# Swin attention and a spiking layer on one core: the softmax's exponentials over both score banks in one operation each

## The reference, cut to what matters

```python
qkv = (part @ qkv_w.T + qkv_b).reshape(n * NW, WS, 3, N_HEAD, HEAD_DIM)
q, k, v = (qkv[:, :, 0] * SCALE, qkv[:, :, 1], qkv[:, :, 2])
attn = jnp.einsum('wihd,wjhd->whij', q, k)
attn = attn.reshape(n, NW, N_HEAD, WS, WS) + bias[None, None] + MASK[None, :, None]
attn = jax.nn.softmax(attn, axis=-1).reshape(n * NW, N_HEAD, WS, WS)
out = jnp.einsum('whij,wjhd->wihd', attn, v).reshape(n * NW, WS, c)
...
x = x + _L0_conv_ref(_gn(x), L0_conv_qkv_w, L0_conv_qkv_b, L0_conv_bias_table)
x = x + _L1_conv_ref(_gn(x), L1_conv_W, L1_conv_b)
```

## Time and profile before

| what | value |
| --- | --- |
| median of 3 runs | 576.61 us (572.59 to 577.72) |
| profiled execution | 574.5 us |
| its span | 572.8 us |
| granted TensorE clock, mean over the span | 0.951 of full speed |

### The profile page before, as it was taken

One profiled execution on the slowest core, in us unless ns is written; L12 is line 12 of the kernel. 1 busy time (PEld: TensorE's weight loads), 2 busy tenths in 40 slices (PEclk: granted clock), 3 DMA queues, 4 the chain that ended last, 5 costly groups with the idle time before them and its releaser, 6 DMA issues.

```text
span 572.8 us, 18181 instructions
## 1 busy us (share of the span) xinstructions
PE 470.8 (82%) x6632; PEld 426.5 (74%) x6632; DVE 464.0 (81%) x995; ACT 434.2 (76%) x1045; POOL 318.1 (56%) x411
## 2 busy tenths in 40 slices
PE   0364699898999899899989998998999778599880
PEld 0364588787888788788878887887888667599770
DVE  6855568888898789888888987898778775779997
ACT  2275679888898899888888988998889567579830
POOL 6133365566555666655566656566555466867630
PEclk9978799999999999999999999999999898889975
DMA  6266066666777677666667776765565450221233
GB/s 185 73 171 160 15 168 173 175 167 181 190 200 192 165 189 180 165 174 170 181 168 196 193 190 167 186 153 150 155 154 153 132 148 3 92 75 74 97 116 137
DMA packets 92577, 86.09 MB, mean 150 GB/s; under 512 B 41842, under 2 KB 63604, under 8 KB 92532
## 3 DMA queue, kind: packets, MB, share of 16 engines
q1 hardware_dynamic: 91808, 85.49, 55.8%
q10 hardware_dynamic: 724, 0.01, 0.1%
HBM read 47.72 MB, written 33.55 MB: 142 GB/s over the span
## 4 chain that ended last, share of the span: by engine, by line
issue 26%; POOL 24%; PE 21%; DVE 11%; ACT 8%; DMA 6%; SPq 2%; POOLq 1%; ACTq 1%; DVEq 0%
POOL p_lo L426 11%; POOL xc L413 5%; POOL xn_lo L386 3%; DVE xc L865 3%; PE pv_ps L1009 3%; DMA k_stack<-k_spill1lo 2%; ACT v_hi L508 2%; DMA k_spill1lo<-k_lo 2%; PE proj_ps L909 2%; PE proj_ps L911 2%; PE proj_ps L910 2%; PE score_ps L986 2%; DVE charged L857 2%; DMA probs<-in_qkv_b_dram 1%; PE max_ps L953 1%
## 5 line engine op out<-in xcount | busy, mean ns | idle before, releaser
L426 POOL TENSOR_TENSOR p_lo<-probs,p_hi 128x512 f16<-128x512 f32 x128 | 146.7, 1167 | 162.6 <-ACT p_hi L587 162.6
L909 PE MATMUL proj_ps<-xn_hi,w_hi 128*128 128x256 f32 x288 | 86.1, 299 | 14.6 <-POOL xn_lo L386 14.0
L763 DVE TENSOR_TENSOR v_lo<-proj_ps,v_hi 64x128 f16<-64x128 f32 x256 | 74.1, 289 | 22.5 <-ACT v_hi L508 19.8
L586 ACT ACTIVATE probs<-score_ps 128x512 f32<-128x512 f32 x128 | 76.9, 601 | 18.1 <-PE score_ps L986 17.3
L976 PE MATMUL score_ps<-both_parts,bias_k 128*128 128x64 f16 x1024 | 82.6, 194 | 6.2 <-DMA k_stack<-k_spill1lo 4.3
L910 PE MATMUL proj_ps<-xn_lo,w_hi 128*128 128x256 f32 x288 | 83.1, 288 | 0.0
L911 PE MATMUL proj_ps<-xn_hi,w_lo 128*128 128x256 f32 x288 | 83.0, 288 | 0.0
L770 DVE TENSOR_REDUCE neg_max<-max_ps 128x16 f16<-128x1024 f32 x64 | 78.4, 1225 | 4.7 <-PE max_ps L959 2.7
L386 POOL TENSOR_TENSOR xn_lo<-xn,xn_hi 128x512 fp32r<-128x512 f32 x48 | 62.5, 1302 | 34.8 <-ACT xn_hi L480 34.7
L978 PE MATMUL score_ps<-q_stack,k_stack 96*128 96x64 f16 x1024 | 81.8, 193 | 0.0
L472 ACT ACTIVATE xn<-xc,shift,rstd 128x256 f32 (+1 forms) x128 | 70.6, 611 | 12.9 <-DVE shift L238 6.6
(11 more groups left out here) (144 smaller groups left out, 1434.9 us busy)
## 6 DMA issues: line engine op xcount, KB each, us to landing
xc<-in_x_dram SPq DMA_DIRECT2D x32, 256.0 KB, 4.9
k_stack<-k_spill0hi SPq DMA_DIRECT2D x32, 256.0 KB, 4.2
k_stack<-k_spill1hi SPq DMA_DIRECT2D x32, 256.0 KB, 4.1
out_dram<-xc SPq DMA_DIRECT2D x32, 256.0 KB, 2.3
q_hi<-q_flat SPq DMA_DIRECT2D x128, 32.0 KB, 2.0
k_spill0hi<-k_hi SPq DMA_DIRECT2D x16, 256.0 KB, 2.2
k_spill0lo<-k_lo SPq DMA_DIRECT2D x16, 256.0 KB, 2.4
q_stack<-q_spill0hi SPq DMA_DIRECT2D x32, 128.0 KB, 2.8
```

What stands on the lines that cost most here:

```text
L426: pool.tensor_tensor(p_lo[p][:, quads, :, :].rearrange("p g w i -> p (g w i)"), probs[:, quads, :, :].rearrange("p g w i -> p (g w i)"), p ...
L586: act.activation(probs[:, quads, :, :].rearrange("p g w i -> p (g w i)"), score_ps[:, h, :], ACT.Exp)
L909: pe.matmul(dst, w_hi[:, c, cols], high[:, tok], start=(c == 0 and bias is None), stop=False)
```

## The change

Each of the two exponentials runs once a pair, over both banks of `score_ps` (1024 columns), in place of once a bank. `p_hi_done` counts pairs, and no longer halves. ACT's exponentials therefore wait for both increments of `score_ps_done`, and for both low parts of the pair before; POOL's first low part waits for the whole f16 exponential; PE's scores of the next pair wait for the whole exponential of this one, for the first bank too. POOL's operations keep their size, two of 512 columns a pair.

```diff
--- before.py
+++ after.py
@@ -421,7 +421,7 @@
                 wait(pool, pv_ps_done, n - 1)
                 for h in range(HALVES):
-                    pool.wait_ge(p_hi_done, n * 2 + (h + 1))
+                    pool.wait_ge(p_hi_done, n + 1)
                     quads = slice(h * QUADS, (h + 1) * QUADS)
@@ -579,13 +579,11 @@
                 wait(act, pv_ps_done, n - 1)
-                for h in range(HALVES):
-                    wait(act, p_lo_done, n * 2 + (h - 1))
-                    act.wait_ge(score_ps_done, n * 2 + (h + 1))
-                    quads = slice(h * QUADS, (h + 1) * QUADS)
-                    act.activation(probs[:, quads, :, :].rearrange("p g w i -> p (g w i)"), score_ps[:, h, :], ACT.Exp)
-                    act.activation(p_hi[p][:, quads, :, :].rearrange("p g w i -> p (g w i)"), score_ps[:, h, :], ACT.Exp)\
-                       .then_inc(p_hi_done, 1)
+                wait(act, p_lo_done, n * 2)
+                act.wait_ge(score_ps_done, n * 2 + 2)
+                both_banks = score_ps[:, :, :].rearrange("p h n -> p (h n)")
+                act.activation(probs[:, :, :, :].rearrange("p g w i -> p (g w i)"), both_banks, ACT.Exp)
+                act.activation(p_hi[p][:, :, :, :].rearrange("p g w i -> p (g w i)"), both_banks, ACT.Exp).then_inc(p_hi_done, 1)
@@ -968,7 +966,7 @@
                 for h in range(HALVES):
-                    wait(pe, p_hi_done, n * 2 + (h - 1))
+                    wait(pe, p_hi_done, n)
                     for g in range(QUADS):
```

## The result

The changed kernel takes 585.67 us (median of 6 runs, 584.07 to 589.08), the kernel before 576.07 in the runs beside it (572.59 to 577.72). The ratio is 1.0187, 95% interval 1.0141 to 1.0234: 1.9% slower, 9.6 us between the medians. (A ratio leaves out every run that is more than 1.5% above the fastest run of its own kernel; here that happened twice, at 590.80 and 590.63 us, both in the kernel with the gap filled.) The profiled execution took 585.46 us, its span 583.7 against 572.8: 10.9 us more. (Behind the two exponentials, lines of the changed kernel carry numbers lower by two: L907 is `project_q`'s first matmul, L701 the root guess.)

What follows compares the result with a forecast made beforehand. Ordinary rows were taken as bound by PE's projections and ACT's `k_hi`, `max_rows`, `v_hi`; changes of sample by POOL's chain. 574.5 + 7.6 (delay) + 4.2 (clock) = 586.3 us, median 2.1 above: 588.4, range 579.5 to 594.5.

Steps and rivals of the forecast that it cites:

- ACT's own time: ACT's exponentials, each pair: two operations of 1.02 us, starts 0.90 apart, save 0.15 us, worth nothing in the cycle.
- The start: Exponentials wait for all 8 maxima matmuls: even pairs start 0.23 us later, inside the slack; odd pairs do not move.
- The three waits with slack: PE's scores, ACT's exponentials and PE's value matmuls, waiting for whole exponentials or both low parts: claimed to cost nothing.
- POOL's start: POOL's `p_lo` starts 1.07 us later; passes through at six changes of sample, 6.4 us, and vanishes in normal rows.
- The first change: First change of sample, under a slow clock: later `p_lo` delays POOL's roots, 0.5 us lost.
- The end: Last pair, whose value matmuls wait for `p_lo`: it starts at 481.03 in place of 480.30, 0.7 us lost.
- The clock: PE's gap before `project_q` grows to 2.4 us; clock falls behind three of six gaps, 1.4 us each, 4.2 us.
- DVE's gain: Root guess at changes of sample runs free of `p_lo`; PE reaches its gap 0.2 us earlier, nothing reaches the end.
- slower in every row: Rival, chance 0.07: two-bank operations cost 1.20 us, even exponentials overrun their slack in every row; 597 us.
- no change: Rival, chance 0.13: POOL's delay is taken up; between 576 and 580 us, given as 577.
- faster: Rival, chance 0.05: ACT is the true bound and each pair gives 0.15 us; some 2 us gained.
- The delay alone: Rival, chance 0.23: POOL's delay costs 7.6 us with no fall of the clock; 584.2 us.

## Why the prediction was right

The forecast was 588.4 us in 579.5 to 594.5, and 11.8 us more than before. Measured are 585.67 and 9.6; against the profiled execution, where the terms were worked out, 11.8 stand against 10.9.

- *What bounds the kernel.* That the exponentials lie beside the cycle of an ordinary row held to the hundredth: 12.78 us before and after.
- *ACT's own time.* 1.02 us forecast, 1.02 measured; starts 0.92 apart for 0.90. The Trainium skill's formula (ScalarE: Activation LUTs, section "What ACT_TABLE_LOAD costs") gives 1.04, 0.02 too much here. The 0.15 us saved went into ACT's idle time ahead of `k_hi`.
- *The start.* 0.23 forecast, 0.22 seen (0.49 to 0.71 us of idle time), and shown by itself to cost nothing in ordinary rows.
- *The three waits with slack.* None came to bear. The 8 matmuls, the value matmuls and the next scores stayed where they were.
- *POOL's start, 6 x 1.07 = 6.4 us.* The six rows without their falls grew by 1.05, 6.3 us. The table above shows that it is a cause.
- *The first change, 0.5 us.* The row of that change went from 15.01 to 15.52, as forecast, but that POOL's delay did it is not shown. PE's wait for `xn_lo` there did not grow but fell from 0.80 to 0.38 us, and the granted clock from 74 to 78 us was 0.82, for 1.00 before: PE itself came later. The same row took 14.21 and 15.48 us in two executions of one kernel, the kernel before with the roots moved, so the agreement may be luck.
- *The end, 0.7 us.* This one failed, by 2.1 us. PE's wait for the last `p_lo` did grow (0.31 us before, 1.35 now), but the part from the start of the last pair's exponentials on became shorter, 92.3 us for 93.7. Two stretches of POOL's timeline show where: the last of the thirteen root operations of the eighth sample and the low part behind it, before and after.

```profile
498.11 0.70 POOL L238 TENSOR_TENSOR shift<-neg_mean,rstd 128x2 f32<-128x2 f32 x1
498.76 1.71 POOL L386 TENSOR_TENSOR unit_lo<-xn,unit_hi 128x512 fp32r<-128x512 f32 x1
```

```profile
510.88 0.52 POOL L238 TENSOR_TENSOR shift<-neg_mean,rstd 128x2 f32<-128x2 f32 x1
511.37 1.26 POOL L386 TENSOR_TENSOR unit_lo<-xn,unit_hi 128x512 fp32r<-128x512 f32 x1
```

  From the first root operation (492.37 and 505.56) to the end of this low part it is 8.10 us before and 7.07 after. These small operations take 0.20 us in the middle of the kernel, and here, where DVE is busy with the membrane, seven of the thirteen took 0.5 to 0.7 before and six after. That their meeting fell out otherwise is how I read it; no run tested it. So 1.0 of the 1.4 us arises between these rows. Over all profiles the end varied from 92.2 to 94.8 us, more than the term in question.
- *The clock, three falls of six at 1.4 us.* Three fell, and each cost 1.4 us (16.81 on average against 15.40). The price was worked out and right; the count was a guess between bounds that came out by luck, since a second execution of the same kernel had four. That the gap causes the falls was shown by filling it.
- *What had no term.* The row behind the wait for DMA at 111.65 us, with its own fall of the clock, added 1.2 us. No step of the forecast had it; it made up for part of the miss at the end, which is luck too.
- *DVE's gain.* The root guess dropped as said, from a median of 0.90 us to 0.17, PE's waits for `neg_max` went, and PE came 0.3 us earlier to its gap (0.2 forecast).

The step from 10.9 between the profiled executions to 9.6 between the medians lies in which executions were profiled: the profiled execution before lay 1.6 us under its median of six, the one after 0.2 us under its own.

Of the rivals, "slower in every row" falls with the ordinary rows at 12.78; "no change" and "faster" with the waits for `xn_lo`, 15.2 us for 7.4. "The delay alone" was half right: with the gap filled, which is that case made by hand, the kernel is 1.1 to 1.2% slower than before by the ratios, 6.4 to 6.9 us, and 10.0 and 8.3 us slower by the medians of all runs; 7.6 was worked out.

## What to carry to other kernels

Merging two operations to save their fixed cost takes a signal away, and the consumer of the first half then starts later by nearly the whole second half; ask for the slack of that consumer in the rarest stretch, not in the usual row. Here all but eight of the 64 pairs had room for 1.07 us, and six of those eight, with the falls of the clock behind three or four of them, make up most of the 1.9%, while the engine that was meant to be relieved became less busy. And a wait of PE that grows can have two prices: its length, and the clock behind it.

## What the runs showed of the hardware

A gap of PE of 0.93 to 1.56 us ahead of the projections was followed by a fall to 1.2 GHz in none of 12 cases (the kernel before, and the later start alone); gaps of 2.00 to 2.61 us in 18 of 30 (five executions). The fall began between 0.6 us ahead of the gap's end and 1.1 us behind it. With 14 matmuls in a gap of 2.49, leaving 0.6, it was 0 of 12. PE's waits for DMA at 111 to 113 us show that length alone does not tell: of the eight of 1.78 to 3.31 us in these profiles six were followed by a fall, but 1.83 in the kernel before was not, 1.84 in the changed kernel was, and 2.06 in the kernel with the f16 exponential in halves was not. Each fall at a change cost 1.3 to 1.5 us of a row, but for one in the kernel with four operations and whole waits, where the slow clock lasted twice as long and the row took 18.08 us.

DVE's two-column operations depend on what POOL does at that moment. The statistics of the root guess, before and after:

```profile
L703 DVE TENSOR_SCALAR root_guess<-tiny x10: 169/896/1135, 18.9 to 490.4; 128x2 int32<-128x2 int32 x9, 128x14 int32<-128x14 int32 x1
```

```profile
L701 DVE TENSOR_SCALAR root_guess<-tiny x10: 169/169/287, 18.8 to 503.6; 128x2 int32<-128x2 int32 x9, 128x14 int32<-128x14 int32 x1
```

And another of them took its place, as the Trainium skill's rule had it in the prediction (SBUF — State Buffer, section "Terms": the loser blocks for a whole instruction), though it met POOL's addition and not `p_lo`. `tiny + moments` at k = 1 went from 0.16 us to a median of 0.58; the case at 288.16 ends at 288.74, just when POOL's addition does (287.99 + 0.74 = 288.73):

```profile
288.16 0.58 DVE L693 TENSOR_TENSOR tiny<-tiny,moments 128x2 f32<-128x2 f32 x1
```

```profile
287.99 0.74 POOL L413 TENSOR_TENSOR xc<-xc,attn_cm 128x256 f32 x1
```

The trace agrees with the rule at both places. It cost nothing here, as DVE had slack at k = 1.
